# A three-layer transformer block on one Trainium2 core: the order of its start, of the gathers and scatters of its second layer, and of the first expert steps there

## The reference, cut to what matters

```python
# x: (8, 512, 128) float32
x = x + attn_a(layernorm(x), W_attn, b_attn, W_proj, b_proj)   # 16 heads of 8, rotary, causal softmax
x = x + ffn(layernorm(x), expert_sel, keys, values)            # top 4 of 64 experts per token
x = x + attn_b(layernorm(x), WQ, WK, WV)                       # one head of 128, band of 64
x = x + ffn(layernorm(x), expert_sel, keys, values)            # the same experts again

def ffn(x, expert_sel, keys, values):
    logits = x @ expert_sel.T
    sel_val, sel_idx = top_k(sigmoid(logits), 4)
    gates = zeros.at[rows, sel_idx].set(sel_val)
    h = einsum('nd,kde->nke', x, keys)
    return einsum('nke,kev->nv', relu(h) * gates[:, :, None], values)
```

## Time and profile before

| | us |
|---|---|
| median of 3 runs | 1250.46 |
| lowest, highest | 1245.94, 1894.88 |
| the profiled execution, its own time | 1248.13 |
| its span | 1246.3 |
| start, to the first scores | 49.5 |
| stage one, to the last attention value product | about 507 |
| stage two with expert steps beside | about 600 to 1040 |
| end stage, gathers and combines of layer two | 1045 to 1246 |

### The profile page before, as it was taken

How to read it: one execution, slowest core, us unless ns; L and a number is a source line. 1 busy time by engine, 2 the same in 40 slices (tenths; PEclk the granted TensorE clock), 3 DMA queues, 4 the chain that set the end, 5 groups by cost and what they waited for, 6 DMA issues and landing times.

```text
span 1246.3 us, 20441 instructions
## 1 busy us (share of the span) xinstructions
PE 872.2 (70%) x6298; PEld 593.3 (48%) x6298; DVE 828.4 (66%) x2421; ACT 485.6 (39%) x1249; POOL 800.4 (64%) x975
## 2 busy tenths in 40 slices
PE   1499988988888887688888876644367677976000
PEld 0133333433433333478787765533267676966000
DVE  3287688889898862566466789986586873654212
ACT  1117655646565454244445532221133344533000
POOL 2214334666766566556799987777775477997774
PEclk9959898989898888698889976665687888988555
DMA  4565453422316231466876631111143466865321
GB/s 127 176 199 180 148 190 111 166 85 78 105 57 208 90 93 60 119 192 194 223 206 181 174 86 49 50 50 51 52 146 105 132 181 187 246 181 163 97 61 53
DMA packets 206538, 163.68 MB, mean 131 GB/s; under 512 B 15968, under 2 KB 191072, under 8 KB 206432
## 3 DMA queue, kind: packets, MB, share of 16 engines
q1 hardware_dynamic: 185696, 112.00, 31.3%
q0 software_dynamic: 16384, 33.59, 8.8%
q10 hardware_dynamic: 4352, 16.78, 3.4%
HBM read 78.94 MB, written 83.36 MB: 130 GB/s over the span
## 4 chain that ended last, share of the span: by engine, by line
PE 36%; POOL 23%; DVE 21%; issue 12%; DMA 4%; SPq 2%; ACT 1%; POOLq 0%; DVEq 0%
POOL v_aug L1624 13%; PE ps L592 7%; PE ps L689 6%; POOL sorted_rows L1611 5%; PE ps L530 4%; PE ps L698 4%; POOL w_attn L1607 3%; PE ps L571 3%; PE ps L678 3%; DVE row_max L1085 3%; DVE x_res L1315 2%; PE ps L557 2%; PE ps L637 2%; PE ps L644 1%; DVE xn L1046 1%
## 5 line engine op out<-in xcount | busy, mean ns | idle before, releaser
L1611 POOL DMA_INDIRECT sorted_rows<-xn,dest x256 | 253.9, 992 | 108.3 <-issue 60.0
L1624 POOL DMA_INDIRECT v_aug<-result_rows,dest x256 | 249.3, 974 | 76.6 <-issue 63.5
L874 ACT ACTIVATE arena<-ps 128x512 f32<-128x512 f32 x320 | 182.9, 605 | 123.3 <-PE ps L530 121.3
L1644 POOL TENSOR_SCALAR_AFFINE_SELECT arena<-arena 128x512 f32<-128x512 f32 (+1 forms) x128 | 64.8, 530 | 173.6 <-ACT arena L874 173.3
L689 PE MATMUL ps<-arena 128*128 128x128 f32 x1024 | 150.3, 294 | 32.8 <-DVE arena L1300 32.5
L557 PE MATMUL ps<-arena 64*128 64x128 bf16 (+3 forms) x576 | 143.5, 312 | 25.9 <-DMA arena<-k_parts 24.6
L1300 DVE COPY arena<-ps 128x512 f32<-128x512 f32 x128 | 88.1, 689 | 108.1 <-PE ps L678 107.9
L689 PEld LDWEIGHTS ps<-arena 128*128 128x128 f32 x1024 | 137.6, 209 | 37.4 <-DVE arena L1300 34.6
L863 ACT COPY arena<-ps 128x512 f32<-128x512 f32 x128 | 75.0, 586 | 205.1 <-PE ps L698 205.0
L1085 DVE TENSOR_REDUCE row_max<-ps 128x1 f32<-128x512 f32 (+1 forms) x192 | 128.1, 683 | 38.7 <-PE ps L571 37.8
L698 PE MATMUL ps<-arena 128*128 x1024 | 143.8, 286 | 2.7 <-ACT arena L863 2.7
(11 more groups left out here) (192 smaller groups left out, 1275.6 us busy)
## 6 DMA issues: line engine op xcount, KB each, us to landing
arena<-sorted_rows SPq DMA_DIRECT2D x128, 256.0 KB, 3.7
result_rows<-arena SPq DMA_DIRECT2D x128, 256.0 KB, 2.7
sorted_rows<-arena ACTq DMA_DIRECT2D x16, 1024.0 KB, 4.3
arena<-q_parts SPq DMA_DIRECT2D x16, 512.0 KB, 4.1
arena<-k_parts SPq DMA_DIRECT2D x16, 512.0 KB, 5.1
q_parts<-parts SPq DMA_DIRECT2D x52, 128.0 KB, 2.5
k_parts<-parts SPq DMA_DIRECT2D x50, 128.0 KB, 2.6
sorted_rows<-xn,dest POOLq DMA_INDIRECT x256, 2.2
```

Source lines behind the costliest of these rows:

```text
L874: nc.scalar.activation(prob[:, grp % 2, pr % 2, PROB_AT[u]:PROB_AT[u] + T], ps[:, v % 3, :], ACT.Exp, scale=SCALE_A).then_inc(exp_done, 1)
L1611: g.indirect_dma_start(sorted_d[b // HALF][:, :], bass.IndirectOffsetOnAxis(dest[:, 16 * b + n:16 * b + n + 1], 0), xn1[:, b % 2, n // TOP ...
L1624: g.indirect_dma_start(yg[:, b % 2, i // TOPK, C * c:C * c + C], None, result_d[layer][b // HALF][:, :], bass.IndirectOffsetOnAxis(dest[:, ...
```

## The change

Four edits. (1) The start: only x of batch 0 and the first four small loads count on in_x and in_w; the other weights count on in_w_later and come ahead of the big load of x, which counts on in_x_rest. DVE takes the statistics of batch 0 first, then rotates the weights, and adds the projected bias later, in `projected_bias`. PE's bias matmul follows the first transpose, and POOL waits for the bias only at its first addition. (2) `write_parts` writes the six slices of parth once act_split allows it, then the four of partm, then the two of partl. (3) In stage two the gather of batch 3 loses its pacing, and in iterations 3 to 5 the scatters come ahead of the gather. (4) `BESIDE` puts seven steps of layer two's half 0 into places 6 to 12 of iteration 6, where eight stood at places 0 to 12, and nine instead of eight into iteration 7.

```diff
-          (1, 0): {6: (1, 0, 1, 1, 0, 1, 0, 1, 1, 0, 1, 0, 1, 0), 7: (1, 0, 1, 1, 0, 1, 0, 1, 1, 0, 1, 0, 1, 0),
+          (1, 0): {6: (0, 0, 0, 0, 0, 0, 1, 1, 1, 1, 1, 1, 1, 0), 7: (1, 0, 1, 1, 0, 1, 1, 1, 1, 0, 1, 0, 1, 0),
...
-            sp.dma_start(x[:, TT:, :], x_d.rearrange("(t p) c -> p t c", p=P)[:, TT:, :]).then_inc(in_x, 16)
-            sp.dma_start(bproj[:, :], bproj_d.unsqueeze(0).broadcast_to([P, C])).then_inc(in_w, 16)
-            for dst, src in ((wproj[:, :], wproj_d), (wb[:, :], wqkv_b_d), (esel[:, :], esel_d)):
-                sp.dma_start(dst, src).then_inc(in_w, 16)
+            for dst, src in ((wproj[:, :], wproj_d), (bproj[:, :], bproj_d.unsqueeze(0).broadcast_to([P, C])),
+                             (wb[:, :], wqkv_b_d), (esel[:, :], esel_d)):
+                sp.dma_start(dst, src).then_inc(in_w_later, 16)
+            sp.dma_start(x[:, TT:, :], x_d.rearrange("(t p) c -> p t c", p=P)[:, TT:, :]).then_inc(in_x_rest, 16)
...
-                sp.wait_ge(act_split, 4 * b + 4)
-                sp.wait_ge(pool_split, 4 * b + 4)
                 if b >= 2:
                     for g in (2 * b - 4, 2 * b - 3):
                         sp.wait_ge(qk_landed[g % 4], 32 * (g // 4 + 1))
-                for d, n, groups in ((qd, 0, (parth, parth, parth, partm, None, partm, partl)),
-                                     (kd, 1, (partl, partm, parth, parth, None, partm, parth))):
-                    for gi, part in enumerate(groups):
-                        if part is not None:
+
+                def write(part, q_rows, k_rows):
+                    for d, n, rows in ((qd, 0, q_rows), (kd, 1, k_rows)):
+                        for gi in rows:
                             sp.dma_start(d[par, :, 8 * gi:8 * gi + 8, :], part[:, n, :]).then_inc(parts_out, 16)
+
+                sp.wait_ge(act_split, 4 * b + 2)
+                write(parth, (0, 1, 2), (2, 3, 6))
+                sp.wait_ge(act_split, 4 * b + 4)
+                write(partm, (3, 5), (1, 5))
+                sp.wait_ge(pool_split, 4 * b + 4)
+                write(partl, (6,), (0,))
...
-            pe.wait_ge(in_w, 16 * 8)
...
-            pe.wait_ge(rotated, 13)
-            pe.matmul(pv[:, 0:C], bvrep, wproj[:, :], start=True, stop=True).then_inc(bias_ready, 1)
...
+                            if (name, it + off) == ("XT", 0):
+                                pe.wait_ge(in_w_later, 16 * 4)
+                                pe.wait_ge(rotated, 13)
+                                pe.matmul(pv[:, 0:C], bvrep, wproj[:, :], start=True, stop=True).then_inc(bias_ready, 1)
...
+
+            def projected_bias():
+                dve.wait_ge(in_w_later, 16 * 4)
                 dve.wait_ge(bias_ready, 1)
...
-            dve.wait_ge(in_w, 16 * 8)
-            dve.wait_ge(in_x, 32)
             dve.wait_ge(consts, NCONST)
-            rotate_weights()
+            dve.wait_ge(in_x, 16)
...
+                            if nxt:
+                                dve.wait_ge(in_x_rest, 16)
...
+                        if nxt == 0:
+                            dve.wait_ge(in_w, 16 * 4)
+                            rotate_weights()
+                    if at == (0, 3) and nxt == 1:
+                        projected_bias()
...
-            pool.wait_ge(in_w, 16 * 8)
...
+                        if b == 0:
+                            pool.wait_ge(rotated, 14)
...
-                if nxt + 1 < B:
-                    gather(0, nxt + 1, paced=paced)
+                if b <= 2:
+                    gather(0, nxt + 1, paced=b < 1)
...
+                if 2 < b < B - 2:
+                    gather(0, nxt + 1, paced=False)
```

More of the change, by code:

```diff
@@ L305, in build @@
         in_w = sem("in_w")
+        in_x_rest = sem("in_x_rest")
+        in_w_later = sem("in_w_later")
         consts = sem("consts")
```

## The result

The changed kernel took 1230.12 us (median of 4 runs, 1229.06 to 1234.63), the kernel before 1251.08 in the same comparison. The ratio is 0.985, its 95% interval 0.981 to 0.990. That is 21 us between the two medians, and some 18 us by the ratio: clear of noise, and just under the 2% that count as a difference. I had forecast 1235. The profiled execution took 1230.66 with a span of 1228.9, where before it was 1248.13 and 1246.3. One run of before at 1894.88 is left out of the ratio, which goes by means, but not out of the median; without it the medians are 20.3 apart.

A forecast was written before the change was run, and what follows sets the result against it. No engine is full; the bound changes by stage: one thread at the start, POOL's gathers and scatters in layer two. Terms -11.3 - 4.2 - 3.6 + 0 + 3.5 + 1.5 = -14.1: span 1232.2, median 1236.4, stated 1235; range 1219 to 1250.

The forecast's parts named there:

- Order of the start: Kernel start: loading and handling batch 0 first ends its normalize at 10.4 instead of 21.76; taken as -11.3 us.
- Slices: Start, SP's twelve slice writes: writing each part once ready ends them at 38.1 instead of 42.28, -4.2 us.
- The two waits for k_parts: Two iterations after the first scores: PE's waits of 1.20 and 2.43 us both go, -3.6 us.
- the start gives back: Rival, early scores: slow-clock stretch grows or something else is late; -7 us, about 1242 (0.20), or about 1246 (0.07).
- Unpaced gather: Layer two, third gather group: 7.0 us off POOL, but POOL idles in place of pacing, so 0 us.
- Scatters ahead of gathers: Layer two, POOL: 9 us of new idling ahead of S1, and G7's later end holds combine 7; +3.5 us.
- steps moved: Layer two, iterations 6 and 7: iteration 6 keeps seven steps after combine, iteration 7 pays for a ninth; +1.5 us.
- The 1.8 us for a step: Layer two, combine to dest: 40.27 us with steps against 27.69 without, 12.6 for seven, 1.8 each.
- Cold steps: Rival, layer two's expert steps: all seven run at the lower clock after idling, +16 us, about 1250; chance 0.10.

The follow-up runs named there:

- start_only: The kernel before with only the new order of the start: 1241.41 us against 1252.57, ratio 0.991.
- slices_only: The kernel before with only the slices written as they come: 1245.34 us, 7.2 less than before, ratio 0.994.
- filled_gap: Changed kernel with the gather first in iteration 3 only, and three of iteration 6's seven steps in place 0: median 1224.36 us, ratio 0.980.
- gather_first: Changed kernel with each gather ahead of the scatters in iterations 3 to 5 again: 1223.43 us, ratio 0.977; repeated, 1227.34 us, ratio 0.982.
- begin_both: The kernel before with the new start and slices, stage two as before: 1228.95 us against 1250.98, ratio 0.982.
- pe_filled: gather_first with 90 matmuls that nobody reads on PE ahead of the first scores: median 1229.37 us, ratio 0.982.

## Why the prediction was right, and where it was wrong

*Order of the start, -11.3.* Right: start_only's scores came 10.6 earlier, and its median was 11.2 lower. The normalize ended at 10.10, for 10.4.

*Slices, -4.2.* Right: 4.5 in slices_only, 14.8 for both where the sum said 15.5.

*The two waits for k_parts, -3.6.* Wrong, and by the mechanism that I gave to a rival ("the start gives back"). The waits went, but the way from the first scores to N didn't get shorter: 232.7 for 231.8, so the term measured +0.8. slices_only, which lost both waits by the slices alone, has 231.8 as well. (The 68.4 that the sum had for the end of the second batch's writes doesn't follow from its rows: two writes behind 64.79 give 66.1, which is what slices_only measured.) In place of the waits the stretch runs longer at the lower level. Before:

```profile
56.21 0.60 PE L557 MATMUL ps<-arena 64*128 64x512 bf16 x1
56.91 0.39 PE L557 MATMUL ps<-arena 64*128 64x512 bf16 x1
...
63.17 0.39 PE L557 MATMUL ps<-arena 64*128 64x512 bf16 x1
...
66.36 0.61 PE L557 MATMUL ps<-arena 64*128 64x512 bf16 x1
```

After, with the scores of iterations -1 and 0:

```profile
61.05 0.61 PE L564 MATMUL ps<-arena 64*128 64x512 bf16 x1
...
82.88 0.61 PE L564 MATMUL ps<-arena 64*128 64x512 bf16 x1
...
86.33 0.39 PE L564 MATMUL ps<-arena 64*128 64x512 bf16 x1
```

Every score of 512 columns took 0.6 us from 34.76 to 82.88; before, they had 0.39 from 56.91 to 63.17, and again from 93.24 on. slices_only's took 0.6 from 45.02 to 85.48 without such a break. From the first score to the first of the next iteration it was 37.6 us before, with 1.2 of waiting (49.53 to 87.13), and 39.7 after, without (34.76 to 74.47).

*What made up for it.* The 4.1 us at the end of stage one, by the clock level, which no step of mine had. Whether the medians have it too isn't shown. In the two profiled executions the span came out 3.3 us under the 1232.2 of the sum: +0.7 from the first scores, +4.4 from the two waits, -4.1 from the end of stage one, -2.8 from stage two (below), and -1.5 in unchanged code (to d0 and to the end). That 1235 was so near is partly luck: a missed term of 4.4 us was covered by a difference between executions of 4.1. On the scale of the runs the sum gave 1236.4, of which I said 1235; the other 3 us under that are of the medians, of which before's lies 2.3 above its profiled execution and the changed kernel's 0.5 below.

*Unpaced gather, 0.* Right, with the 7 us back as idling (8.92 ahead of G4, for 0.86).

*Scatters ahead of gathers, +3.5, and steps moved, +1.5.* The mechanism was right: S1 waits 9.24 us, G7 ends last and holds combine 7. On the scale of d0 I had put combine 7 at 911.4 - 751.65 = 159.8; it was 157.0, and before 156.2. So the term measured +0.8. The six groups from S1 took 125.1 us, 20.9 each, not 21.25, and that is 2.4 of the 2.7. From combine to d5 it was 41.25 for 40.27, +1.0 where the sum had 0, so d5 came 1.8 late from d0 and not 3.5. The +1.5 of the steps was to be paid in iteration 7; from d5 to d7 it measured +0.4. Together +2.2 for +5.0. The 1.8 us for a step, from which this term came, isn't borne out: filled_gap shows some 0.5.

What the step did miss is that the two edits don't add. I priced each against before, where early steps hid behind the wait for S3. Against the right partner, the gather first with late steps, the changed order costs 7.0 us (198.3 for 191.2).

*Cold steps.* The rival fell: the lower level came for the first step alone (1.06 us for four transposes at 902.50, then 0.60 at 906.69), where before the first two had it (1.09 at 904.80, 1.06 at 908.97).

**The best version found** by the way from d0 to d5 is filled_gap (189.0 us), then gather_first (191.2 and 190.9), where the changed kernel has 198.3 and 198.6. By the times no choice is shown: gather_first has ratios of 0.977 (0.975 to 0.979) and, again, 0.982 (0.979 to 0.986) to before, filled_gap 0.980 (0.976 to 0.984), the changed kernel 0.985 and 0.983 (0.980 to 0.987).

## What to carry to other kernels

Price two edits of one stage together: one that moves a wait and one that fills it may each be worth something only with a certain form of the other, and four kernels of a cross show it. Where an in-order engine idles, work fills the gap only if it stands ahead of the wait in that engine's stream, and on every engine that the work passes through. Judge an order of a few us between two landmarks that stand close around it in the trace; medians of whole runs carry the scatter of all other stages.

## What the runs showed of the hardware

The record of the granted clock and the matmuls' own times disagree at the start. After's window of 60 to 70 us:

```profile
60.00:70.00 10.00, 10.00 (x37) 4.18 (x36) 7.67 (x19) 0.69 (x2) 1.02 (x1) 1.00 0.72 267
```

It says 1.00 with PE busy throughout, and the scores in it take 0.61 us; begin_both, with the same scores at 0.61, says 0.50. Elsewhere 0.39 goes with 1.00. The Trainium skill, "TensorE: Matmul & The Clock Gate", section "Seeing it yourself", warns that the records of the clock gate have been seen to be unreliable; here the durations decide. By them PE stayed at its lower level (1.2 GHz) for 48 us of nearly full work (34.76 to 83.5), and for at least 41 us in begin_both (34.55 to 75.6), which I had not expected. In pe_filled the 90 matmuls had reached the upper level, but with 7 us of idling behind them the scores began at the lower one and, but for some 3 us, had it to 74.6 at least. So full work lifted the level in the one stretch and for long not in the other, and no run here shows why.
